# A cleared tile behind each indirect transfer of GpSimd, in a two-layer network with routed experts

## The reference

```
x = layernorm(x + attention(x))          # 16 heads, causal, latent keys and values
x = layernorm(x + experts64(x))          # router, top 8 of 64 experts, at most 128 tokens each
x = layernorm(x + recurrence(x))         # gated scan over 1024 steps, plus a gated local part
x = layernorm(x + experts8(x))           # router, top 2 of 8 experts, plus a shared part

# experts64
pos = cumsum(one_hot(topi)) - 1          # a token's place in its expert
xe[expert, pos] = x                      # rows sent to their experts (pos < 128)
ye = (silu(xe @ gate) * (xe @ up)) @ down
y[token] = sum_k weight[token, k] * ye[expert_k, pos_k]
```

## Time and profile before

| | |
|---|---|
| median of 3 timed runs | 817.85 us |
| the profiled execution, first to last instruction | 851.6 us, TensorE's granted clock 0.982 |
| PE busy | 786.6 us (92%) |
| POOL busy | 271.2 us (32%) |
| of it 64 sends L708, 64 scatters home L738 | 64.1 and 61.4 us |
| of it 16 sends L777, 16 gathers L783 | 15.8 and 15.3 us |
| stage of the 64 experts, first scatter home to the end of the last | 436.03 to 551.27 us |

### The profile page before, as it was taken

How to read it: one execution, slowest core, us unless ns; L and a number is a source line. 1 busy time by engine, 2 the same in 40 slices (tenths; PEclk the granted TensorE clock), 3 DMA queues, 4 the chain that set the end, 5 groups by cost and what they waited for, 6 DMA issues and landing times.

```text
span 851.6 us, 16159 instructions
## 1 busy us (share of the span) xinstructions
PE 786.6 (92%) x4635; PEld 660.7 (78%) x4635; DVE 556.9 (65%) x1423; ACT 394.8 (46%) x898; POOL 271.2 (32%) x357
## 2 busy tenths in 40 slices
PE   8998999999899999999879998899999799999957
PEld 7887877778787887777677877788897688888746
DVE  4324778877778787777345555468856387778536
ACT  1334656656565666655123343323333266666411
POOL 2004445534333232222345545524415100000241
PEclk9999999999999999999889999999999999999979
DMA  7449950000000000073176999687621335555321
GB/s 212 102 107 384 406 198 34 34 27 27 21 27 28 20 21 14 27 240 135 51 230 184 323 319 296 213 288 257 246 99 69 106 112 150 149 149 153 95 69 49
DMA packets 62881, 120.74 MB, mean 142 GB/s; under 512 B 18272, under 2 KB 32864, under 8 KB 62688
## 3 DMA queue, kind: packets, MB, share of 16 engines
q1 hardware_dynamic: 51824, 95.41, 35.2%
q0 software_dynamic: 7680, 21.51, 7.0%
q10 hardware_dynamic: 3312, 3.02, 1.0%
HBM read 76.13 MB, written 43.78 MB: 141 GB/s over the span
## 4 chain that ended last, share of the span: by engine, by line
PE 65%; DVE 11%; issue 11%; ACT 4%; POOL 3%; another core or an unknown queue 3%; DMA 2%; DVEq 0%; SPq 0%; ACTq 0%; POOLq 0%
PE scores L1627 9%; PE scores L1625 8%; PE scores L1626 8%; PE scores L1849 5%; PE acc_ps L2035 4%; PE misc_ps L1755 3%; PE probsT_ps L1762 3%; PE probsT_ps L1740 3%; PE misc_ps L1753 3%; DVE xT_lo L1096 3%; PE scores L1859 3%; PE acc_ps L1740 2%; PE probsT_ps L1979 2%; DVE neg_max L1090 2%
## 5 line engine op out<-in xcount | busy, mean ns | idle before, releaser
L826 ACT ACTIVATE area<-scores,neg_max 128x128 f32<-128x128 f32 (+7 forms) x128 | 94.9, 742 | 87.7 <-DVE neg_max L1090 85.5
L1090 DVE TENSOR_REDUCE neg_max<-scores 128x1 f32<-128x128 f32 (+7 forms) x128 | 95.8, 750 | 22.1 <-PE scores L1712 20.8
L708 POOL DMA_INDIRECT xe_d<-x_rows,send_i x64 | 64.1, 1001 | 55.5 <-ACT x_rows L850 38.5
L738 POOL DMA_INDIRECT ye_d<-area,home_i x64 | 61.4, 959 | 58.7 <-issue 28.6
L1849 PE MATMUL scores<-area 128*96 128x128 f32 x512 | 69.1, 279 | 2.1 <-issue 1.3
L1625 PE MATMUL scores<-kT_hi,weff_hi 128*128 128x512 f32 (+3 forms) x172 | 66.8, 388 | 0.9 <-ACT area L803 0.4
L1849 PEld LDWEIGHTS scores<-area 128*96 128x96 f32 x512 | 60.5, 166 | 5.2 <-issue 2.7
L1627 PE MATMUL scores<-kT_hi,weff_lo 128*128 128x512 f32 (+3 forms) x172 | 61.7, 359 | 0.0
L1626 PE MATMUL scores<-kT_lo,weff_hi 128*128 128x512 f32 (+3 forms) x172 | 61.5, 358 | 0.0
L696 POOL CAST weff_hi<-area 128x256 fp32r<-128x256 f32 x42 | 17.0, 406 | 136.5 <-PE scores L1712 88.8
L1755 PE MATMUL misc_ps<-xT_lo,xT_hi 128*128 128x512 f32 x144 | 58.4, 406 | 2.2 <-DVE xT_lo L1096 2.1
(11 more groups left out here) (290 smaller groups left out, 2081.4 us busy)
## 6 DMA issues: line engine op xcount, KB each, us to landing
area<-w SPq DMA_DIRECT2D x23, 512.0 KB, 4.0
area<-gate_up SPq DMA_DIRECT2D x24, 384.0 KB
xe_d<-area SPq DMA_DIRECT2D x8, 1088.0 KB, 11.3
ye_d<-area SPq DMA_DIRECT2D x8, 1024.0 KB, 16.7
area<-w SPq DMA_DIRECT2D x8, 1024.0 KB, 7.2
area<-ye_d SPq DMA_DIRECT2D x15, 512.0 KB, 5.2
area<-xe_d SPq DMA_DIRECT2D x28, 272.0 KB
area<-down SPq DMA_DIRECT2D x24, 192.0 KB
```

What stands on the lines that cost most here:

```text
L826: act.activation(row_of(n)[:, 0:L], score_bank(n)[:, 0:L], ACT.Exp, bias=neg_max[:, n % 4:n % 4 + 1], accum_out=rsum[:, s, k:k + 1]).then_ ...
L1090: dve.tensor_reduce(neg_max[:, n % 4:n % 4 + 1], score_bank(n)[:, 0:(n // HEADS + 1) * P], AX.X, ALU.max, negate=True).then_inc(max_ready, 1)
```

## The change

A helper `keep_apart` clears a spare tile of 128x256 numbers, `pause`, which nothing reads, and waits for that clearing to be done. It is called behind each send of tiles 6 and 7, behind each of the 64 scatters home, behind each of the 16 sends to slots, and behind each of the 16 final gathers.

```diff
+        pause = sb("pause", [P, HID])
...
+        paused = sem("paused")
...
+            pauses = [0]
+
+            def keep_apart():
+
+                pauses[0] += 1
+                pool.memset(pause[:], 0.0).then_inc(paused, 1)
+                pool.wait_ge(paused, pauses[0])
+
             def send(t, k):
...
                                         None).then_inc(sent[k % 2] if t < TILES - 1 else sent_last[k], 16)
+                if t >= TILES - 2:
+                    keep_apart()
...
                 pool.indirect_dma_start(ye_d, bass.IndirectOffsetOnAxis(home_i[:, u:u + 1], 0),
                                         ye[:, u, :], None).then_inc(moved[u], 16)
+                keep_apart()
...
                     pool.indirect_dma_start(xd_d, bass.IndirectOffsetOnAxis(slot1[:, t, k:k + 1], 0),
                                             x1[:, t, :], None).then_inc(sent1, 16)
+                    keep_apart()
...
                     pool.indirect_dma_start(last_rows[:, t, k, :], None, yd_d,
                                             bass.IndirectOffsetOnAxis(slot1[:, t, k:k + 1], 0)).then_inc(moved[t], 16)
+                    keep_apart()
```

## The result

| | before | after |
|---|---|---|
| timed runs, median (range) | 817.58 us (814.3 to 819.14, 4 runs) | 874.77 us (872.91 to 877.3, 4 runs) |
| ratio, 95% interval | | 1.071 (1.0682 to 1.0738) |
| span of the profiled execution, mean granted clock | 851.6 us; profiled once more: 816.0 us, 0.993 | 875.5 us, 0.975 |

The change costs 57.2 us. The forecast was 867.0, a loss of 49.1, and the time lies inside its range.

A forecast was written before the change was run, and what follows sets the result against it. Took TensorE, at 1.53 us an expert, to bound the experts' stage, with GpSimd taking over at 2.16 us; 42.7 (experts) + 4.4 (slots) + 2.0 (gathers) = 49.1 us on 817.85 gives 867 us, range 831 to 882.

The forecast's parts named there:

- The stalls: Idle time at dense runs of indirect transfers in the first profile, read as belonging to that execution, not the timed runs.
- a sum of 33 to 35 us: Stalls on the path: experts 17.9 plus 3.9 at start, slots about 2.9, tail 8.2 to 10.6; profile-to-timed difference 33.8.
- The rivals at 849, 833 and 793 us: Stalls in timed runs: staying, 849 (0.15); broken up by clearings, 833 (0.10); removed with preparation hidden, 793, faster (0.05).
- The clearing, 0.31 us: All 112 places: one clearing of 256 columns takes GpSimd 0.31 us, starting when the transfer ends.
- The gap of 0.89 us for the scatters home: Experts' stage: 0.89 us from clearing's end to next scatter, taken from ScalarE's copy to the scatter waiting for it.
- the 0.15 us: Lower bound for the gap, where a transfer follows an ordinary operation without such a wait; gives a 1.42 us period.
- The period of 2.16 us: Scatters home: 0.96 + 0.31 + 0.89 us each against TensorE's 1.53, making GpSimd the stage's bound; +42.7 us with its start.
- The start of the scatters home: Last tile's sends take 1.56 instead of 1.26 us, so scatters home begin at 434.5 instead of 431.5.
- Slots: The 16 sends to slots: 0.30 us more each over 15 intervals, with the last clearing, +4.4 us.
- Gathers: The 16 final gathers: landed at 826.7 against VectorE's last-tile sum at 824.7 without the stall, +2.0 us.
- The clock rival, 920 us: Experts' stage: TensorE, 71% busy, falls to its lower clock, 2.98 us an expert, another 53 us; chance 0.05.
- The rule that was weighed: Trainium skill: waiting instructions enter a hardware queue while the next is decoded, so preparation hides and the change is nearly free.

The follow-up runs named there:

- home alone: The change with clearing and wait kept only behind the 64 scatters home: 853.96 us against 816.86 before, ratio 1.0489.
- all but home: The change without clearing and wait at the scatters home, kept at the other 48 places: 834.89 us, ratio 1.0242 to before.
- no increments: The change with no increment between a clearing's wait and the next transfer (holds as plain waits, last tile's signal earlier): 830.79 us, ratio 1.0195 to before.
- one column: The whole change, but each clearing writes one column instead of 256: 851.71 us against 816.12 before, ratio 1.0441.
- late-wait kernel: The change's 112 clearings, each wait moved directly ahead of the next transfer, behind its other waits and increments: 837.56 us, ratio 1.0265 to before.
- before again: The unchanged kernel profiled a second time: span 816.0 us, 818.1 us for the profiled run.
- plain waits: The kernel before, no clearings, with the two holds ahead of each scatter home made plain waits: 816.4 us against 816.12, ratio 1.0003.

## Why the prediction was right, and where it was off

**The stalls.** The reading that they belong to the profiled execution, taken from a sum of 33 to 35 us against 33.8, is borne out: 816.0 us without them. The sum itself was less sure than it looks: the 2.9 us of the slots and the 10.6 of the tail stand in no row. Stage by stage, the first profile of before is longer than the second by 9.3 us up to the first scatter home (3.9 in the sum; 5.3 of them lie ahead of the last tile's sends), 14.6 in the experts' stage (17.9), 4.3 for slots and blocks (2.9) and 11.0 from the gathers on (8.2 to 10.6), and shorter by 3.6 between the stage and the slots. The total agrees better than its parts. The rivals at 849, 833 and 793 us rested on stalls in the timed runs and fall with it.

**The clearing, 0.31 us.** Measured 0.326, and each one serial.

**The gap of 0.89 us for the scatters home.** Measured 0.91 to 0.93. The row of before that was preferred to the 0.15 us showed the very mechanism: a wait, then an increment, then a transfer whose preparation starts late. The period of 2.16 us was 2.21 as a rule and 2.24 on average, since some gaps are longer (1.24 at the last). The base was not 1.53 but 1.58 us: 1.53 is an expert that follows the last at once, and 63 of them hold some longer ones. The two errors, 63 x 0.08 = 5.0 and 63 x 0.05 = 3.2, mostly cancel, +41.5 against +39.7; that the stage came out so close is in part luck. The way back to TensorE is another than forecast: not ScalarE's copy but VectorE's computation of the weights and homes waits for the scatters of eight experts earlier (36.9 us in 25 waits). The bound is the same.

**The start of the scatters home.** This is the term that was most mis-sized: +3.0 forecast, +8.1 measured. The prediction said that "the sends have two waits and no increments", and gave the last tile's sends 0.29 us behind the wait. It is `sem_inc(last_sends)` that stands there, and the gap is 0.88. Seven intervals of 2.23 instead of 1.27 us are 6.7 us, and 0.6 stand before the first scatter home. The remaining 0.8 us lies ahead of these sends (416.9 instead of 416.1); in the profiles of home alone, all but home and no increments they began at 414.6, 417.4 and 414.9, so it may be no effect at all.

**Slots.** +4.1 against +4.4. What was left out is the next thing on the path. TensorE waits longer for the rows, and what follows runs at the lower clock. From TensorE's timeline, after, then before (second profile):

```profile
700.76 0.69 PE L2003 MATMUL misc_ps<-ident,area 128*128 128x128 f32 x2 [5.35 <-DMA area<-xd_d]
701.24 5.49 PE L1994 MATMUL probsT_ps<-area 128*128 128x256 f32 x16
```

```profile
648.49 0.44 PE L1988 MATMUL misc_ps<-ident,area 128*128 128x128 f32 x2 [1.30 <-DMA area<-xd_d]
648.77 3.62 PE L1979 MATMUL probsT_ps<-area 128*128 128x256 f32 x16
```

The same 16 matmuls take 1.9 us more, most of the +2.3 us in the blocks. The kernel with one column shows the dip after 2.55 us of idle time already, with +2.1 us in the blocks, and the second profile of before shows none after 1.30 us.

**Gathers.** +2.0 forecast, +4.9 measured. The last tile's sum starts 26.7 us after the first gather instead of 23.2, so +3.5: the gathers end 5.1 us later, and VectorE, which in the second profile of before started 3.3 us behind the last gather, now starts 1.8 behind it and waits for the landing. The slack is 1.6 us. The forecast had put it at 2.5 (VectorE at 824.7, the landing at 822.2), and three small errors add up to the 1.5 us: the gathers end 5.1 us later, not 4.5; they land 1.8 us after the last gather, not 1.3; and VectorE without the stall starts 3.3 us behind the last gather, not 3.8. Another 1.4 us is the clock. VectorE's and TensorE's rows after, then before (second profile), beside the earlier trace rows:

```profile
857.74 0.48 DVE L1575 SCALAR_TENSOR_TENSOR area<-area,weight,x_rows 128x256 f32<-128x256 f32 x1 [2.04 <-DMA area<-yd_d,slot]
...
862.57 8.58 PE L1994 MATMUL probsT_ps<-area 128*128 128x256 f32 x32 [5.17 <-DVE area L1588]
```

```profile
799.65 0.48 DVE L1560 SCALAR_TENSOR_TENSOR area<-area,weight,x_rows 128x256 f32<-128x256 f32 x1
...
804.48 7.17 PE L1979 MATMUL probsT_ps<-area 128*128 128x256 f32 x32 [1.12 <-DVE area L1573]
```

**The clock rival, 920 us.** In the experts' stage the clock averages 0.95, not 1.00, so it does fall at times. In the chain above eight matmuls take 1.52 and 1.51 us and their starts (499.66, 502.47) stand 2.8 us apart, more than GpSimd's 2.21. But only one interval between scatters grew there, to 2.52 us (501.07 to 503.59), and the next eight matmuls take 1.1 and then 1.0 us again. The rival took the 2.98 us of the start for a lasting state; it was not one.

**The rule that was weighed.** The gap in the change is 0.91 to 0.93 us at the scatters home, not the short one, so the rule quoted from the Trainium skill (Perfetto Trace Analysis, DMA Instruction — SWDGE) did not decide this case. The runs show where it does: 0.28 us where the transfer is the one that waits. The same page has the other half, which I had not brought in (Sequencer-only Instruction): such an instruction waits in the sequencer itself, and the next is decoded only once it has executed. The long gap where an increment holds the wait, the short one where the transfer does, and the increments of the late-wait kernel, done a scatter ahead, agree with the two read together. What fills the 0.74 us is not shown; the traces record nothing in it.

## What to carry to other kernels

Ask of every wait on the engine that issues transfers which instruction does the waiting. Here a wait held by the transfer itself costs 0.28 us, one that stops the queue ahead of it 0.8 to 0.9, and what decides may be an increment of 0.02 us in between, or the order of the waits. Put such increments ahead of the wait, and let the transfer hold the wait for what ends last: in these kernels it holds the first of the plain waits written ahead of it. Such a gap costs nothing while another engine sets the period and everything once the sum passes it: 0.97 + 0.33 + 0.28 = 1.58 us was free here, 0.97 + 0.33 + 0.92 cost 41.5 us in the stage. And before terms are taken from a profile, hold its span against the timed runs, since stalls of one execution look like part of the kernel.

## What had not been expected of the hardware

- The gap before an indirect transfer behind a finished producer on the chip: 0.28 us when the transfer waits itself (home in the late-wait kernel and in the one without increments; slots and gathers of the change); 0.88 to 0.93 where an increment ahead of the transfer holds the wait; 0.81 where the wait stands with another in an instruction ahead of the transfer; 0.16 to 0.23 when the wait had long been met.
- One profiled execution was 35.6 us longer than its repeat and held waits put down to something remote (31.5 us on ScalarE, 9.5 on VectorE, in part at the same time); none of the nine others did, two of them (before again, plain waits) with the transfers as dense on average or denser. The cause stays open.
- After 5.35 us without work TensorE's next 16 matmuls took 5.49 us instead of 3.62, with a granted clock of 0.77 over the window, and after 5.17 us 32 matmuls took 8.58 instead of 7.17. After 2.55 us (one column) 16 took 5.31, after 1.30 us (second profile of before) 3.62. The 4.1 us at the slots cost 6.4 so, with the blocks behind them.
